# Recurrence: next chunk's tokens turned in steps 13 and 14; token shift and first mixing input of chunk 0 made in the last two steps of the first MLP

## The reference

```
xa = _ln(x, ln1_w, ln1_b)
sx = jnp.concatenate([state[:, 1:2] - xa[:, :1], xa[:, :-1] - xa[:, 1:]], axis=1)
xxx = jnp.tanh((xa + sx * maa_x) @ maa_w1).reshape(b, l, 5, DM)
xxx = jnp.einsum('blfd,fde->blfe', xxx, maa_w2)
xm = xa[:, :, None] + sx[:, :, None] * (maa_stack + xxx)
xk, xw, xv, xr, xg = (xm[:, :, j] for j in range(5))
w = jnp.exp(-jnp.exp(time_decay + jnp.tanh(xw @ td_w1) @ td_w2)).reshape(b, l, h, s_)
r = (xr @ Wr.T) ...; k = (xk @ Wk.T) ...; v = (xv @ Wv.T) ...; g = silu(xg @ Wg.T)
...
def step(s, rkvw):
    a = k_t[..., :, None] * v_t[..., None, :]
    out = jnp.einsum('bhi,bhij->bhj', r_t, u * a + s)
    s = a + w_t[..., :, None] * s
    return (s, out)
```

## Time and profile before

| | before |
|---|---|
| median of 3 runs (lowest to highest) | 1966.96 us (1965.16 to 1967.43) |
| the profiled execution, its time | 1965.55 us |
| its span in the trace | 1963.7 us |
| PE, DVE, ACT, POOL busy | 95%, 57%, 53%, 51% of the span |
| first MLP's last down block ends, first scan step begins on DVE | about 363.4 and 396.1 us |
| scan steps | 396 to 636 us |

### The profile page before, as it was taken

One profiled execution on the slowest core, in us unless ns is written; L12 is line 12 of the kernel. 1 busy time (PEld: TensorE's weight loads), 2 busy tenths in 40 slices (PEclk: granted clock), 3 DMA queues, 4 the chain that ended last, 5 costly groups with the idle time before them and its releaser, 6 DMA issues.

```text
span 1963.7 us, 37702 instructions
## 1 busy us (share of the span) xinstructions
PE 1864.4 (95%) x14320; PEld 1510.1 (77%) x14320; DVE 1114.4 (57%) x2104; ACT 1042.8 (53%) x1945; POOL 1000.6 (51%) x1140
## 2 busy tenths in 40 slices
PE   7999999988897899999999999999999998999899
PEld 5777789534454688888888888888888887977788
DVE  4566656389989555444454444454444455755654
ACT  3565543333343655666666656556666654345542
POOL 6777741366663644645544544545444534347630
PEclk9999999889998999999999999999999999999999
DMA  6000010000000322322233332232332310010000
GB/s 237 2 2 2 2 57 1 1 1 1 1 1 2 112 77 80 93 89 90 85 95 91 89 100 83 86 103 82 94 93 84 96 56 1 22 34 12 2 12 33
DMA packets 61841, 108.01 MB, mean 55 GB/s; under 512 B 7008, under 2 KB 42336, under 8 KB 60256
## 3 DMA queue, kind: packets, MB, share of 16 engines
q1 hardware_dynamic: 60784, 103.38, 16.9%
q10 hardware_dynamic: 880, 2.22, 0.3%
HBM read 103.47 MB, written 2.10 MB: 54 GB/s over the span
## 4 chain that ended last, share of the span: by engine, by line
PE 82%; DVE 8%; issue 4%; POOL 3%; ACT 2%; DMA 0%; DVEq 0%; SPq 0%; ACTq 0%; POOLq 0%
PE banks L865 18%; PE banks L936 9%; PE banks L893 9%; PE banks L630 7%; PE banks L647 7%; PE banks L469 7%; PE banks L925 6%; PE banks L906 3%; PE banks L478 3%; PE banks L551 2%; PE banks L526 2%; PE banks L508 2%; PE banks L537 2%; PE banks L914 1%; PE banks L463 1%
## 5 line engine op out<-in xcount | busy, mean ns | idle before, releaser
L1984 POOL TENSOR_TENSOR w_lo<-w2ring,w_hi 128x512 fp32r<-128x512 f32 x128 | 180.5, 1410 | 245.1 <-ACT w_hi L1131 245.1
L1808 DVE TENSOR_REDUCE nmax<-banks 128x4 f32<-128x260 f32 x128 | 54.2, 424 | 309.5 <-PE banks L906 309.5
L2067 POOL TENSOR_TENSOR wo_lo<-wo_ring,wo_hi 128x256 fp32r<-128x256 f32 x128 | 93.2, 737 | 250.8 <-ACT wo_hi L1339 250.7
L1796 DVE TENSOR_TENSOR v<-banks,dbv 128x512 f32<-128x512 f32 x128 | 88.6, 692 | 158.6 <-PE banks L893 158.6
L1339 ACT ACTIVATE wo_hi<-wo_ring 128x256 fp32r<-128x256 f32 x128 | 53.2, 417 | 191.0 <-PE banks L936 190.1
L936 PE MATMUL banks<-wo_hi,c_hi 128*128 128x256 f32 x512 | 149.1, 291 | 4.7 <-DVE c_lo L1801 4.4
L936 PE MATMUL banks<-wo_lo,c_hi 128*128 128x256 f32 x512 | 146.4, 286 | 0.0
L936 PE MATMUL banks<-wo_hi,c_lo 128*128 128x256 f32 x512 | 146.3, 286 | 0.0
L1326 ACT ACTIVATE k<-banks,cols 128x512 f32<-128x512 f32 x128 | 88.1, 689 | 80.5 <-PE banks L865 80.4
L925 PE MATMUL banks<-PT,v 128*128 128x128 f32 x1024 | 124.7, 275 | 1.0 <-issue 0.8
L925 PEld LDWEIGHTS banks<-PT,v 128*128 128x128 f32 x1024 | 119.7, 192 | 1.6 <-issue 1.2
(11 more groups left out here) (235 smaller groups left out, 5446.0 us busy)
## 6 DMA issues: line engine op xcount, KB each, us to landing
w2ring<-in_w SPq DMA_DIRECT2D x128, 384.0 KB, 3.2
b2ring<-in_b SPq DMA_DIRECT2D x128, 128.0 KB, 3.9
wo_ring<-in_wo SPq DMA_DIRECT2D x128, 128.0 KB, 3.3
mlp_w<-in_mlp SPq DMA_DIRECT2D x6, 1024.0 KB, 7.3
wl<-in_wres SPq DMA_DIRECT2D x1, 2688.0 KB, 8.9
X<-in_x_in SPq DMA_DIRECT2D x4, 512.0 KB, 11.1
wb<-in_wres SPq DMA_DIRECT2D x2, 1024.0 KB, 10.8
ctxT<-in_ctx_in SPq DMA_DIRECT2D x4, 512.0 KB, 18.8
```

The source lines that it names most:

```text
L1796: V.tensor_tensor(v2[i], held(("v2", v, i)).rearrange("p (s d) -> p s d", s=HV), dbv, ALU.add).then_inc(S["l2_v"], 1)
L1984: G.tensor_tensor(w2_lo[:, n % 2, :], w2ring[:, n % HR, 0:2 * KT * P], w2_hi[:, n % 2, :].bitcast(f32), ALU.subtract).then_inc(S["l2_wlo"], 1)
L2067: G.tensor_tensor(wo_lo[:, n % 2, :], wo_ring[:, n % WR, :], wo_hi[:, n % 2, :].bitcast(f32), ALU.subtract).then_inc(S["l2_wolo"], 1)
```

## The change

The next item's halves are turned in scan steps 13 and 14 (and lead-in steps 13 and 14) in place of 14 and 15, on PE and on ACT. The lead-in now begins at j = 2 on every engine, and its pieces 0 and 1, the token shift and first mixing input of chunk 0, are issued by DVE and POOL in the last two steps of the first MLP. PE and ACT have nothing in pieces 0 and 1.

```diff
+FIRST_PIECES = 2
@@ tensor, rwkv
-                    for j in range(NS):
+                    for j in range(FIRST_PIECES, NS):
                         before(0, j)
-                        if j >= 14:
-                            front(L1_FIRST + 1, j - 14, MIDDLE)
+                        if j in (13, 14):
+                            front(L1_FIRST + 1, j - 13, MIDDLE)
                         yield 1
...
-                            if j >= 14:
-                                front(L1_FIRST + c + 2, j - 14, MIDDLE)
+                            if j in (13, 14):
+                                front(L1_FIRST + c + 2, j - 13, MIDDLE)
@@ scalar, rwkv: the same two edits
@@ vector, mlp
                         if i == 5 and c + 1 < CHUNKS:
                             split(it + 1)
+                        if m == 0 and n >= CHUNKS * MT - FIRST_PIECES:
+                            before(0, n - CHUNKS * MT + FIRST_PIECES)
                         yield 1
```

More of the change, by code:

```diff
@@ L1247, in rwkv @@
                             normed(L1_FIRST + 1)
-                        if j >= 14:
-                            front(L1_FIRST + 1, j - 14)
+                        if j in (13, 14):
+                            front(L1_FIRST + 1, j - 13)
                         yield 1
@@ L1264, in rwkv @@
                                 normed(L1_FIRST + c + 2)
-                            if j >= 14:
-                                front(L1_FIRST + c + 2, j - 14)
+                            if j in (13, 14):
+                                front(L1_FIRST + c + 2, j - 13)
                         else:
```

## The result

The changed kernel takes 1953.61 us (median of 4 runs, 1952.69 to 1954.40) against 1966.59 us of the kernel before on the same chip (4 runs, 1965.16 to 1967.43): the ratio is 0.9935, with a 95% interval from 0.9917 to 0.9952. The profiled execution took 1953.34 us, its span is 1951.5.

The account below looks back on a forecast made before the run. DVE was taken to bound the scan steps, held at two seams by a PE and ACT chain. Seams 4.0 plus lead-in 3.9 off the median 1966.96 gave 1959.1 us, range 1954.5 to 1966.0.

Parts of the forecast that it names:

- What bounds the kernel: Recurrence: DVE bounds the scan steps, PE's use, front and ACT's hT hold it at two seams; gains there reach the end.
- Part 1, the seams: Seams between chunks: moving two groups of four transposes earlier removes DVE's waits ahead of the token shift, 4.0 us won.
- The three amounts for the waits: At the first, second and third seams between chunks: 2.1, 1.7 and 0.2 us won.
- 2.35 + 2.37 + 0.74 = 5.5 above: Seams: upper bound of 5.5 us on their gain, from DVE's two idle stretches and its wait for the first state.
- the sum: Whole kernel: 4.0 from seams and 3.9 from the lead-in, 7.9 us off the median 1966.96, giving 1959.1 us.
- the clock behind the lead-in: Recurrence after the lead-in: the prediction has no term for a changed clock there.
- the range: Whole kernel's time: 1954.5 to 1966.0 us for 8 in 10.
- Part 2, the lead-in: Stretch ahead of the recurrence: 3.9 us won if the clock stays up, 0.5 lost with the clock as before.
- the new wait of 2.0: Lead-in ahead of z: PE newly idles 2.0 us, from 355.52 to 357.5, with no down block left there.
- the clock that stays up: Lead-in, windows 366 to 377: TensorE's clock stays at its upper level because PE is busier there, at 6 in 10.
- from `mix(0, 0)` to the first `use` it is 4.6: Lead-in: this stretch through DVE and POOL keeps its earlier 4.6 us, so that use starts at 368.6.
- The rivals: Clock falls in lead-in, chance 0.27; seams do not pay, 0.13; nothing comes of it, 0.09; slower, 1972.5 us, 0.06.

Follow-up runs that it names:

- experiment 11: Kernel before the change, with chunk 3's mix in step 8 made twice over to fill most of PE's 1.37 us wait: 1963.10 us, ratio 0.9985.
- experiment 4: Kernel before the change, with POOL's step-1 product waiting until DVE's first mixing input of the next chunk is done: 1962.84 us, ratio 0.9984.
- experiment 8: Changed kernel, with one PE down block ahead of z, one between z and mixes, one behind them, and DVE's last update later: 1954.39 us.
- experiment 13: Changed kernel, with PE's last down block behind mix(0, 1) and POOL's step-1 product waiting for DVE's next first mixing input: 1955.61 us.
- experiment 5: Changed kernel, with only PE's lead-in blocks placed as before the change; DVE, ACT and POOL keep the early pieces: 1955.78 us, ratio 0.9943.
- experiment 7: Kernel before the change, with three unread products added on PE behind mix(0, 1): 1963.08 us, ratio 0.9981.
- experiment 6: Changed kernel, with PE's last down block moved behind mix(0, 1) so the two mixes are neighbours: 1952.50 us, ratio 0.9927.
- experiment 1: Changed kernel with the seams part alone, its lead-in beginning at j = 0 as in the kernel before: 1957.43 us, ratio 0.9954.
- experiment 3: The changed kernel again, unaltered, on the same chip as its two parts: 1952.77 us, ratio 0.9935.
- experiment 12: Changed kernel, with one unread product added on PE ahead of the lead-in's first use: 1956.52 us, ratio 0.9949.

## Why the prediction was right and wrong

*What bounds the kernel.* Right: DVE paces the scan steps, PE's chain holds the seams, and all that was won by the last scan reached the end.

*Part 1, the seams.* The three amounts for the waits are right: 2.15 for 2.1; 1.7 for 1.7 (5.21 sooner at step 18, 4.78 at step 32, 6.92 at step 33: the 2.1 less the 0.4); and 0.2 for 0.2 (1.93 between steps 45 and 55, of which 1.70 come without it in experiment 11). **One step that failed is the bound "2.35 + 2.37 + 0.74 = 5.5 above".** It took the wait that goes away for the most that the edit can bring, and the rest of the step for unchanged. At two seams DVE's pair lost POOL's product as a neighbour, 1.0 each [experiment 4]. The Trainium skill (SBUF — State Buffer, SBUF: two separate sides) says that DVE and GpSimd take the pair of ports that they share as an exclusive lock, held for a whole instruction by whichever starts first, when DVE's operation has two inputs in SBUF and GpSimd's reads SBUF. The trace agrees in that both are longer while they overlap: 2.40 in place of 1.39 for the pair, and 1.69 in place of 1.27 for the product; it does not show the ports. The row of 2.40 stood in the trace of the kernel before, and I did not ask why the same two instructions took 1.41 in the lead-in the earlier trace rows and 2.40 here.

*The clock inside the recurrence.* **The other step that failed, and the larger, is that the sum puts the clock behind the lead-in at nothing, without a reason.** The prediction looked at the clock only in the lead-in, where it expected a change; but any edit that moves the recurrence by some microseconds also moves its waits, and in this change the low stretches near steps 41 and 52 went away: 3.3 us [experiment 11]. Without it the sum would be 1958.0, well inside the range; with it, it is 1954.7, at the low end. The 1.7 near step 41 went this way and not the other by luck; experiments 8 and 13 show the same stretch come back with 1.7 to 1.8 lost. For the 1.6 near step 52 luck is not shown: it came with the new fronts every time, so they may be what brings it, but no run tests that.

*Part 2, the lead-in.* The mechanism was right, from the new wait of 2.0 to the clock that stays up, with the reason given (PE is busier where it used to wait) shown by experiments 5 and 7. The size was 3.9 for 3.0: the last activation of the MLP came 0.91 later (from 354.29 to 355.20, out of the stages ahead), the first scan 2.07 earlier. The term that failed is "from `mix(0, 0)` to the first `use` it is 4.6": with a block between them the mixes cost 1.98 each, and it is 5.44; with the block moved away it is 4.64 [experiment 6]. The new wait of 1.97 ahead of z was followed by no fall: the clock is at 1.00 in every window from 356 to 378.

*The sum.* 7.9 forecast, less 0.9 for the lead-in, plus 2.0 for the pairs, plus 3.3 for the clock: 12.3. The profiled execution is 12.21 shorter; that this fits so closely is chance, since the 0.9 of the later MLP is made up for by some tenths in several places (0.4 behind the last scan among them).

*The rivals.* None came. The seams paid in full, the clock did not fall in the lead-in, and no new wait of PE took their place. There was no rival in which the change brought more than its terms.

What stays open is what decides whether the clock falls in a given wait near steps 41 and 52, and for how long. In the one run that covered the wait the fall did not come [experiment 11]. Kernels with the same wait of 1.36 to 1.38 have the fall or not: the changed kernel has none, experiments 1 and 6 a short one, experiments 8 and 13 a long one. When the wait ends does not decide it alone: it ends at 527.93 in experiment 3, without a fall, and at 527.87 in experiment 13, with one. I can't forecast it from a trace of the kernel before.

## What to carry to other kernels

Ask of each instruction of the pacing engine what it costs alone and what it costs here: a pair at 2.40 that takes 1.41 elsewhere is a gain that waits for any edit that moves its neighbour. Where TensorE waits among narrow products (here 1.37 and 2.60 us), price the work behind the wait at both clocks, for the places behind the edit too, and put work that has to be done anyway (here an MLP block) into the wait; then look at later waits too, since the low stretches there can move (experiments 7, 8, 12). Compare kernels at a fixed landmark of the pacing engine, step by step: the times alone would have given the seams 9.1 us, of which some 6 are shown to be theirs.

## What the hardware did that I had not expected

- Narrow products in different rows of the array run side by side only while they are neighbours in PE's program. `mix(0, 0)` has both products in the first 32 rows of the array, `mix(0, 1)` in the next 32. A `mix` of two products shows as four instructions in the trace. As neighbours the eight instructions take 1.99 us together; with a `down` block between them four take 1.98 and four take 1.98. `mix(0, 2)`, whose own two products lie in two such groups of rows, takes 1.13. The Trainium skill (TensorE: Matmul & The Clock Gate, The mechanism) states that tiles in different row groups overlap; the trace agrees.
- Work that is thrown away made the kernel faster twice: three products in the lead-in (3.9 us less) and one mix made twice over (3.2 us less). In both traces the clock stays up over the wait that was filled; behind the first, other low stretches moved as well.
- A wait added on POOL, which holds it for 1.45 us, made the kernel 3.7 us faster. Of these, 3.0 are three of DVE's pairs that no longer run beside POOL's product.
- A low stretch of the clock costs between nothing and 1.8 us near step 41, by what it meets. At 525.0 to 528.4 it was over before the `use` and cost nothing (experiment 12); at 527.9 to 534.7 it made a `use` of 3.70 take 5.85 (experiment 8).
